# Gate weights of both token tiles turned in one transpose, their bias products in two row groups and two banks

## What is computed

```python
gates = jax.nn.softmax(xf @ gW + gb, axis=-1)
top2_scores, top2_idx = jax.lax.top_k(gates, 2)
w = (one_hot(top2_idx, 8) * top2_scores[..., None]).sum(1)      # (tokens, 8)
h = relu(einsum('nd,edf->enf', xf, W1) + b1[:, None, :])
y = einsum('enf,efd->end', h, W2) + b2[:, None, :]
out = einsum('ne,end->nd', w, y)
```

## Time and profile before

| | |
|---|---|
| median of 3 runs | 2332.45 us (2331.99 to 2336.62) |
| profiled execution, its own time | 2339.04 us |
| span of that execution | 2337.2 us |
| TensorE busy | 2125.1 us, 91% |
| TensorE weight loads | 1617.7 us, 69% |
| VectorE busy | 1713.5 us, 73% |
| ScalarE busy | 1460.4 us, 62% |
| GpSimd busy | 818.8 us, 35% |
| mean granted TensorE clock | 0.966 of full speed |

### The profile page before, as it was taken

One profiled execution on the slowest core, in us unless ns is written; L12 is line 12 of the kernel. 1 busy time (PEld: TensorE's weight loads), 2 busy tenths in 40 slices (PEclk: granted clock), 3 DMA queues, 4 the chain that ended last, 5 costly groups with the idle time before them and its releaser, 6 DMA issues. The chain is left out here.

```text
span 2337.2 us, 47534 instructions
## 1 busy us (share of the span) xinstructions
PE 2125.1 (91%) x16832; PEld 1617.7 (69%) x16832; DVE 1713.5 (73%) x4415; ACT 1460.4 (62%) x3129; POOL 818.8 (35%) x1204
## 2 busy tenths in 40 slices
PE   4878889999999999999999999999999999997766
PEld 2556667777777777776777777776777777775544
DVE  6666878787887878787887878787787878654432
ACT  3555657667675767767575766767575766754323
POOL 5112333334343333434343333434343333423131
PEclk9989999999999999999999999999999999998777
DMA  5020112121202112121202112120211212111010
GB/s 151 4 53 11 45 42 54 42 56 41 50 18 43 46 42 56 42 54 31 46 25 51 47 42 57 42 54 15 51 37 42 56 42 53 36 48 38 10 41 5
DMA packets 255196, 100.59 MB, mean 43 GB/s; under 512 B 118553, under 2 KB 253857, under 8 KB 254401
## 3 DMA queue, kind: packets, MB, share of 16 engines
q1 hardware_dynamic: 254960, 97.55, 17.2%
HBM read 51.12 MB, written 46.14 MB: 42 GB/s over the span
## 5 line engine op out<-in xcount | busy, mean ns | idle before, releaser
L1176 DVE SCALAR_TENSOR_TENSOR work<-psA,c_conv_w,work 128x255 f32<-128x255 f32 (+2 forms) x810 | 329.3, 472 | 15.1 <-ACT work L916 14.2
L1251 DVE TENSOR_REDUCE nmax<-psB 128x2 f32<-128x512 f32 x512 | 315.9, 678 | 26.5 <-PE psB L733 26.2
L601 PE MATMUL psA<-xnT_a,c_w_in 128*128 128x256 f32 x1088 | 306.3, 406 | 26.2 <-ACT X L940 15.0
L1203 DVE TENSOR_TENSOR att<-att,QK 128x1024 f32<-128x1024 f32 x192 | 235.4, 1253 | 85.0 <-ACT att L953 84.8
L835 PE MATMUL psB<-c_w,hid 128*128 128x128 f32 x2048 | 279.7, 281 | 8.1 <-ACT pt L999 6.7
L835 PEld LDWEIGHTS psB<-c_w,hid 128*128 128x128 f32 x2048 | 256.9, 193 | 42.3 <-issue 19.4
L999 ACT ACTIVATE pt<-psB 128x512 f32<-128x512 f32 x512 | 264.4, 606 | 32.8 <-PE psB L752 32.8
L825 PE MATMUL psB<-x1T,c_w 128*128 128x256 f32 x1024 | 276.4, 398 | 5.0 <-ACT hid L1041 4.8
L953 ACT ACTIVATE att<-psA 128x512 f32<-128x512 f32 x384 | 204.5, 610 | 110.1 <-PE psA L642 83.0
L1022 ACT ACTIVATE hid<-psB,c_b 128x256 f32<-128x256 f32 x512 | 217.2, 483 | 56.4 <-PE psB L825 52.5
L601 PEld LDWEIGHTS psA<-xnT_a,c_w_in 128*128 128x128 f32 x1088 | 192.8, 199 | 70.6 <-ACT X L940 23.8
(11 more groups left out here) (245 smaller groups left out, 4272.7 us busy)
## 6 DMA issues: line engine op xcount, KB each, us to landing
qk_scr<-qparts SPq DMA_DIRECT2D x192, 192.0 KB, 2.5
q_stack<-qk_scr SPq DMA_DIRECT2D x32, 576.0 KB
k_stack<-qk_scr SPq DMA_DIRECT2D x32, 576.0 KB
lvl_scr<-work SPq DMA_DIRECT2D x32, 192.0 KB, 5.1
low<-lvl_scr SPq DMA_DIRECT2D x256, 1.5 KB
c_w_in<-in_in_wT SPq DMA_DIRECT2D x1, 2176.0 KB, 8.7
x<-in_x SPq DMA_DIRECT2D x16, 128.0 KB, 4.4
c_w<-in_W SPq DMA_DIRECT2D x2, 1024.0 KB
```

The source lines that it names most:

```text
L601: e.matmul(t[:, 0:T], w_in[:, first + j * P:first + (j + 1) * P], xnT_a[:, :], start=True, stop=True).then_inc(filled[b], 1)
L1176: m = e.scalar_tensor_tensor(out=cv[:, back:], in0=t[:, 0:T - back], scalar=conv_w[:, c, tap:tap + 1], in1=cv[:, back:], op0=ALU.mult, op1 ...
L1203: e.tensor_tensor(att[:, :, :], att[:, :, :], bc(QK[:, kq, :], 1, HG), ALU.mult).then_inc(att_done, 1)
L1251: e.tensor_reduce(nmax[:, i, 2 * h2:2 * h2 + 2], t[:, :].rearrange("p (h k) -> p h k", k=T), AX.X, ALU.max).then_inc(drained[b], 1)
```

## The change

The gate weights of both tiles are kept 32 columns apart (`WE_STEP`), so that one transpose of 40 columns yields tile 0's eight rows at partitions 0 to 7 and tile 1's at partitions 32 to 39, 128 columns wide. `b_2` is loaded twice, at partitions 0 to 7 and 32 to 39, with zeros between. The two products read partitions 0 to 7 and 32 to 39 of both and write two banks in place of two halves of one; `experts` step 1 now takes two banks. The copy on ScalarE is 40 rows by 128 columns, and VectorE's add is done in two instructions, one for each bank. `acc` 0 waits for the second. The columns between the gate weights are set to zero once for each lay.

```diff
 SLOTROWS = 96
+WE_STEP = 32
+WE_ROWS = WE_STEP + NE
@@ banks_of
     if what == "experts":
-        return 1, int(k < 2)
+        return 1, (1, 2, 0, 0)[k]
@@
-        b_2 = load("b_2", [NE, HID], d["b2"])
+        b_2 = load("b_2", [WE_ROWS, HID], d["b2"])
@@
-        w_e_b = [sb(f"w_e{i}", [P, NT, NE]) for i in range(2)]
-        w_eT = sb("w_eT", [NE, T])
+        w_e_b = [sb(f"w_e{i}", [P, NT, WE_STEP]) for i in range(2)]
+        w_eT = sb("w_eT", [WE_ROWS, P])
@@ tensor
-                    e.transpose(t[0:NE, 0:P], w_e_b[lay][:, 0, :], ident[:, :])
-                    e.transpose(t[0:NE, P:T], w_e_b[lay][:, 1, :], ident[:, :]).then_inc(filled[b], 1)
+                    e.transpose(t[0:WE_ROWS, 0:P], w_e_b[lay][:, :, :].rearrange("p i c -> p (i c)")[:, 0:WE_ROWS],
+                                ident[:, :]).then_inc(filled[b], 1)
                 elif what == "experts" and k == 1:
-                    t, b, u = bank(hop)
                     e.wait_ge(*empty(("experts", lay, n, 0)))
-                    if u:
-                        e.wait_ge(drained[b], u)
-                    e.matmul(t[:, 0:P], w_eT[:, 0:P], b_2[:, :], start=True, stop=True)
-                    e.matmul(t[:, P:T], w_eT[:, P:T], b_2[:, :], start=True, stop=True).then_inc(filled[b], 1)
+                    for i in range(NT):
+                        t, b, u = bank(hop, i)
+                        if u:
+                            e.wait_ge(drained[b], u)
+                    for i in range(NT):
+                        t, b, u = bank(hop, i)
+                        r = i * WE_STEP
+                        e.matmul(t[:, 0:P], w_eT[r:r + NE, :], b_2[r:r + NE, :], start=True, stop=True).then_inc(filled[b], 1)
@@ scalar
-                    e.activation(w_eT[:, :], t[0:NE, 0:T], ACT.Copy).then_inc(drained[b], 1)
+                    e.activation(w_eT[:, :], t[0:WE_ROWS, 0:P], ACT.Copy).then_inc(drained[b], 1)
@@ vector
-                    w_e = w_e_b[lay]
+                    w_e = w_e_b[lay][:, :, 0:NE]
+                    if n == 0:
+                        e.memset(w_e_b[lay][:, :, NE:WE_STEP], 0.0).then_inc(*own.step())
@@
                 elif what == "experts" and k == 1:
-                    t, b, u = bank(hop)
-                    e.wait_ge(filled[b], u + 1)
-                    e.tensor_tensor(ff_b[lay][:, :, :], t[:, 0:T].rearrange("p (i c) -> p i c", c=HID), x1_b[lay][:, :, :],
-                                    ALU.add).then_inc(drained[b], 1)
+                    for i in range(NT):
+                        t, b, u = bank(hop, i)
+                        e.wait_ge(filled[b], u + 1)
+                        e.tensor_tensor(ff_b[lay][:, i, :], t[:, 0:P], x1_b[lay][:, i, :], ALU.add).then_inc(drained[b], 1)
@@
-                    e.wait_ge(*(empty(("experts", lay, n, 1)) if k == 0 else empty(("down", lay, n, k - 1))))
+                    e.wait_ge(*(empty(("experts", lay, n, 1), 1) if k == 0 else empty(("down", lay, n, k - 1))))
@@ host
+        "b2": np.concatenate([a[pf + "b2"], np.zeros((WE_STEP - NE, HID), np.float32), a[pf + "b2"]]),
```

More of the change, by code:

```diff
@@ L1506, in lay_out @@
         "b1_cols": f(a[pf + "b1"].reshape(-1, P).T),
-        "W2": f(a[pf + "W2"].reshape(-1, P, HID).transpose(1, 0, 2)), "b2": a[pf + "b2"],
+        "W2": f(a[pf + "W2"].reshape(-1, P, HID).transpose(1, 0, 2)),
+        "b2": np.concatenate([a[pf + "b2"], np.zeros((WE_STEP - NE, HID), np.float32), a[pf + "b2"]]),
     }
```

## The result

The changed kernel took 2343.33 us (median of 8 runs, 2338.55 to 2355.55), against 2332.22 (8 runs) for the kernel before on the same chip: a ratio of 1.0043, 95% interval 1.0027 to 1.0058. It is slower, by 11.1 us on the medians. The profiled execution took 2355.55 us, with a span of 2353.7, 16.5 more than the profiled one of before.

What follows compares the result with a forecast made beforehand. TensorE, busy 91% of the span, was taken to set the pace, except at lay 1's late VectorE add. Wait +13.1, savings -3.2 and -0.6, clock falls +9.8 gave +19.1 us: 2351.5 for the median, range 2337 to 2364.

Steps and rivals of the forecast that it cites:

- The sign and the cause: Slower, as lay 1's down1.0 waits for VectorE's first add once experts1.1 takes two banks: 1.0 us a turn.
- the main case: Lay 1's wait for the add plus clock falls after seven of 13 waits: 2346 to 2358 us, chance 0.55.
- the case without falls: Rival: the same wait at down1.0 but no clock falls, +9.3 us, 2341.8 (2338 to 2346), chance 0.25.
- The products' term: Two row groups on TensorE: one pair of passes overlaps, saving 0.11 us a hop, between bounds 0 and 0.22.
- the second bank of es1.2: Lay 0: it waits a little for ocopy1.1, so lay 0 gains 0.1 to 0.3 us a hop, 0.2 taken.
- The stall: Lay 1: down1.0 starts 1.92 us late, rowmax0.3 1.01 late, so 13 turns lose 1.01 us each, +13.1.
- Nothing gives it back: After lay 1's wait TensorE is packed, so the 1.0 us delay a turn stays.
- The clock: After TensorE's 1.97 us idle stretch before down1.0, half-rate falls follow seven of 13 waits at 1.4 us: +9.8.
- The sum: Wait +13.1, lay 0 -3.2, lay 1's three turns without wait -0.6, clock +9.8: +19.1 us.
- The faster one: Rival: slack after 1180 of a turn takes the delay up again, -3.8 us or so, 2328.6, chance 0.06.
- That the row groups don't overlap: Rival inside the main case: the products' passes stay apart, 1.8 us more than forecast, 2353.3; no own chance.
- a fall after every wait: Rival: the clock falls after all 13 waits at full price, +31.4 us, 2363.9 (2358 to 2366), chance 0.10.

Runs made afterwards that it cites:

- experiments 3 and 6: On the changed kernel, VectorE's adds made earlier: 3, experts1.1 ordered ahead of coef0.0, ratio 0.9933; 6, lay 1's adds done before mix1.8's product, 0.9938.
- experiment 1: The change made in one lay only, the other as in the kernel before: lay 0 alone 0.9949, lay 1 alone 1.0087 against the kernel before.
- the repetition: The changed kernel as it is, run again on another group's chip: 2358.5 us, 1.0068 against the kernel before.
- the two filled kernels: The changed kernel with mix1.10's product before down1.0 computed four times (2343.8 us, 1.0026) or twice (2342.4 us, 1.0014), against the kernel before.
- experiment 5: The changed kernel with mix1.10's product computed four times (1.0026) or twice (1.0014), and the changed kernel run again (1.0068), against the kernel before.
- the three kernels with the full wait: The changed kernel (2343.33 us), the kernel before with the change in lay 1 alone (2359.2), and the changed kernel run again (2358.5).
- experiment 2: The kernel before with two banks and two adds, keeping two transposes and one row group: 2356.2 us, 1.0066 against the kernel before.

## Why the prediction was right, and where it wasn't

**The sign and the cause were right.** down1.0 waits for the first add in 13 steady turns, for 2.09 us, where 1.97 was forecast; without it, or with a quarter of it left, the same change is faster than before (experiments 3 and 6), and so is the change in lay 0 alone (experiment 1). The number was less so. By the prediction's own division, 2343.33 lies not in the main case (2346 to 2358) but in the case without falls (2338 to 2346), although the falls did come.

**The products' term was mis-sized.** The prediction took 0.11 a hop and gave 0.22 as the bound, on the argument that a queue worked off in order can overlap only one pair of passes. In the trace the four passes start at 0, 7, 213 and 220 ns, and the next matmul at 0.42 (1486.64 and 1487.06 above), where before they started at 0, 213, 325 and 437 ns, and the next at 0.64 (from 1073.37 to 1074.01). The argument was wrong: each pass of one product goes beside the pass of the other, and the pair of products costs 0.22 less. The rule of the Trainium skill (TensorEngine Tiling, Key Properties) that tiles work in parallel was the better forecast. With the transpose's 0.11 that is 0.33 in place of 0.2 for lay 0, 5.3 us a run. All of it arrives there: the second bank of es1.2 does wait for ocopy1.1, as forecast, by 0.26 us, but the hop behind, down1.7, starts 1.65 after the products where before it started 1.87 after them.

**The stall came out a little larger.** smax0.3's first score starts 1.90 later after the products than before (6.41 against 4.51), of which VectorE's rowmax keeps 1.26 (1493.47, 6.83 after the products, against 5.57). The products are 0.11 earlier by the saved transpose, so 1.15 is left, against 1.01. Of the excess, 0.09 is the release: down1.0 starts 0.43 after the first add began, where 0.28 + 0.06 was taken. Its first weight load starts at 1491.18, 0.11 after the add's end, and the matmul 0.04 behind the load. The other 0.05 isn't traced.

**"Nothing gives it back" held, with luck in its number.** A stall of 1.15 less lay 0's 0.33 leaves 0.82 a turn, where 1.01 - 0.2 = 0.81 was forecast: two terms were too small by about the same. In the profile after, the four turns at full clock are only 0.57 longer than before's, but only one of the four has the long form of the six-column addition, against eight of nine in before, and that is worth 0.28 (at 0.44 a turn, experiment 1). With the repetition and the two filled kernels of experiment 5, which have the wait at the same place, 28 turns at full clock are 0.79 longer on average. What the prediction missed is an instruction whose length depends on when GpSimd starts, which moves a turn by as much as a saving does.

**The clock was right in kind and number.** Seven falls of 13 were forecast; 6, 6 and 7 of 13 came in the three kernels with the full wait. That it was seven is in part luck: it was chosen below the five of seven in the fill, and no row gave it. A turn with one such fall is 134.6 to 135.8 long, against 133.3 on average; over the three kernels the 15 such turns are 1.4 longer on average than their own kernel's at full clock, as forecast. A second fall in a turn, away from the wait, gave 136.0 to 136.4. Over the profiled run the steady turns hold ten falls against three in before.

**The sum.** In the profiled run the twelve steady turns are 19.3 us longer than before's: 12 x 0.57 = 6.9 at full clock, and 12.4 from falls (the eight turns with ten falls are 15.3 longer than they would be at full clock, the three of before with one each 2.9). Fill and drain are 2.8 shorter, which makes 16.5, against 19.1 forecast. On medians it is 11.1. The term that doesn't carry over is the falls. The profiled run is the longest of the eight, with a mean granted clock of 0.960, where the other seven have 0.962 to 0.970; the four runs at 0.966 or less took 2344.02 to 2355.55, the four above 2338.55 to 2342.64. The forecast gave every run seven more falls; by their clocks, most runs had fewer than the profiled one. The forecast of 2351.5 missed by 8.2 us, and the measured time lies 1.5 above the rival without falls, 2341.8. It lies within the range because the range takes in that rival. The repetition in experiment 5 was 18.8 us above before on medians and 1.0068 in ratio, so two groups of the same kernel differ by almost as much as the forecast missed by.

**The rivals.** The faster one (the delay is taken up after 1180 of a turn) fell: turns at full clock stay longer. That the row groups don't overlap fell too, more clearly than thought. Of the two on the clock, neither "no falls" nor "a fall after every wait" came: it was about half of the waits.

## What to carry to other kernels

A saving that needs one more bank of a ring is paid by the hop that now looks one place less far back; look up which engine drains that place and how late it comes, for each place where the step runs. If it comes late, move the draining instruction ahead in its own engine's queue, or put a hop of another ring into the wait, before giving up the saving. Two products eight rows deep in different row groups run side by side in both their passes: 0.42 us in all here, where in one row group they took 0.64 and each pass more cost 0.11, so about as much as one product (an estimate from these).

## What the runs showed of the hardware

**Idle stretches and the clock.** TensorE's idle stretch ahead of down1.0 and the falls to the half level in the five microseconds after it, by kernel: 2.09 us: 6, 6 and 7 of 13; 1.82 to 1.84 (experiment 2): 0 of 13; 1.66: 0; 1.23: 0; 0.80: 0. Nineteen of 39 at 2.09, none of 52 at 1.84 and less. Between 2.09 and 1.66 nothing but the filling differs; the kernel of 1.82 to 1.84 also has other slots ahead of the wait. A fall made a turn 1.4 us longer on average. Idle stretches aren't the whole of it: the steady part of before has none above 0.92 us, and three falls. These, and all but one of the falls away from the wait in the other kernels, began 121.6 to 125.0 us after lay 1's products. Of the nine waits of 2.09 us that came within 23 us after a fall away from the wait, eight were followed by a fall of their own, of the other 30 eleven. Why 2.09 brings a fall in some turns and not in others stays open.

**VectorE beside GpSimd.** Besides the six-column addition, ccoef (128x64, both inputs in SBUF, ahead of the add) is another case. Its line in before:

```profile
L1195 DVE TENSOR_TENSOR ccoef<-ccoef,c_d_skip x16: 224/704/711, 68.9 to 2008.5; 128x64 f32<-128x64 f32 x16
```

It takes 0.22 in the first two turns, where GpSimd isn't at its mix sums (L1461) yet, and 0.70 to 0.71 in the other 14, beside them. So 0.48 of the add's lateness would come from GpSimd (an estimate from the difference). A way that takes the sums out of ccoef's reach wasn't tried.

**Row groups.** A pair of f32 products of 8 rows, at partitions 0 and 32, takes 0.42 from its first start to the next matmul's. Loading 40 columns takes 100 ns against 87 for 8 (median of 32 each), and costs nothing that shows: in lay 0 the products start 1.20 after the transpose where they started 1.31 after the first of two, so the whole slot of 0.11 is saved.
